# A quantised feed-forward kernel with batch-wise projection: projecting on 128 rows instead of 64, turning the weights before they are rounded, and new programs for all engines

## The reference

```python
def reference(x, itok, cond_weights, w_up, w_down):
    w = cond_weights[itok]                          # (64, 64, 64)
    z = einsum('bct,bcd->bdt', x, w)                # per sample
    h = hbitlinear(z, w_up)                         # 512 -> 1024
    h = square(relu(h))
    return x + hbitlinear(h, w_down)                # 1024 -> 512

def hbitlinear(x, w):
    x = fwht(x)                                     # Walsh-Hadamard over the last axis, / sqrt(n)
    scale = 127 / max(abs(x).max(-1), 1e-5)         # one scale per token
    xq = clip(round(x * scale), -127, 127) / scale
    s = max(mean(abs(w)), 1e-5)
    wq = clip(round(w / s), -1, 1) * s              # ternary weights
    return einsum('bsd,fd->bsf', xq, wq)
```

## Time and profile before

| | |
|---|---|
| time, median of 3 runs | 283.66 us (283.53 to 283.95) |
| the profiled execution, its span | 279.9 us |
| TensorE busy | 246.1 us (88%) |
| VectorE busy | 204.7 us (73%) |
| GpSimd busy | 181.4 us (65%) |
| ScalarE busy | 147.4 us (53%) |
| DMA moved | 34.96 MB in 67369 packets, mean 125 GB/s |

### The profile page before, as it was taken

One profiled execution on the slowest core, in us unless ns is written; L12 is line 12 of the kernel. 1 busy time (PEld: TensorE's weight loads), 2 busy tenths in 40 slices (PEclk: granted clock), 3 DMA queues, 4 the chain that ended last, 5 costly groups with the idle time before them and its releaser, 6 DMA issues.

```text
span 279.9 us, 6739 instructions
## 1 busy us (share of the span) xinstructions
PE 246.1 (88%) x2116; PEld 203.6 (73%) x2116; DVE 204.7 (73%) x341; ACT 147.4 (53%) x193; POOL 181.4 (65%) x231
## 2 busy tenths in 40 slices
PE   0266899799999999999999999999999899985872
PEld 0266797797979797979797888888888687754441
DVE  0145557799888697888878796969697977887632
ACT  2143588765647465655656565556462766641220
POOL 1333133869797979697979788887976467278510
PEclk9999999999999999999999999999999999998899
DMA  6865963245563745585664437434443325553364
GB/s 188 305 210 204 191 158 51 42 122 95 143 107 92 154 122 89 143 143 128 155 191 87 122 75 215 94 94 98 116 84 106 81 57 109 135 112 75 75 86 141
DMA packets 67369, 34.96 MB, mean 125 GB/s; under 512 B 57490, under 2 KB 57618, under 8 KB 67346
## 3 DMA queue, kind: packets, MB, share of 16 engines
q10 hardware_dynamic: 52432, 14.75, 28.4%
q1 hardware_dynamic: 14914, 19.93, 23.3%
HBM read 13.70 MB, written 8.39 MB: 79 GB/s over the span
## 4 chain that ended last, share of the span: by engine, by line
PE 61%; issue 9%; DMA 8%; POOL 6%; DVE 5%; ACTq 4%; ACT 3%; SPq 2%; POOLq 0%; DVEq 0%
PE u_ps L750 15%; PE h_ps L737 14%; PE o_ps L761 13%; PE y_ps L708 10%; PE z_ps L721 8%; DMA zqT<-zq 4%; POOL p L422 4%; ACTq L527 2%; DMA uqT<-uq 2%; ACT uq L547 2%; POOL u_deq L430 1%; DVE u_max L931 1%; ACTq L554 1%; DVE y L893 1%; DMA w_pair<-in_L_cond_weights_dram 1%
## 5 line engine op out<-in xcount | busy, mean ns | idle before, releaser
L422 POOL TENSOR_TENSOR p<-g 128x512 f32<-128x512 f32 x64 | 80.9, 1287 | 23.6 <-DVE g L924 22.9
L750 PEld LDWEIGHTS u_ps<-had_sb,p 128*128 128x128 f32 x512 | 61.0, 193 | 12.2 <-POOL p L422 7.1
L750 PE MATMUL u_ps<-had_sb,p 128*128 128x128 f32 x512 | 63.8, 278 | 6.8 <-POOL p L422 4.4
L737 PE MATMUL h_ps<-zqT,w_upT 128*128 128x256 f16 x512 | 61.8, 272 | 2.5 <-ACT g L534 1.3
L761 PE MATMUL o_ps<-w_downT,uqT 128*128 128x512 f16 x256 | 61.7, 384 | 2.4 <-DMA uqT<-uq 2.4
L385 POOL TENSOR_TENSOR x_half<-x_all 128x512 f32<-128x512 f32 (+1 forms) x32 | 40.9, 1300 | 25.9 <-PE y_ps L708 15.3
L737 PEld LDWEIGHTS h_ps<-zqT,w_upT 128*128 128x128 f16 x512 | 49.4, 98 | 9.5 <-issue 2.0
L547 ACT ACTIVATE uq<-u_ps,u_mul 128x1024 f16<-128x1024 f32 x32 | 35.6, 1114 | 34.2 <-DVE u_mul L944 28.2
L534 ACT ACTIVATE g<-h_ps 128x512 f32<-128x512 f32 x64 | 37.7, 595 | 21.8 <-PE h_ps L737 10.1
L931 DVE TENSOR_REDUCE u_max<-u_ps 128x1 f32<-128x1024 f32 x32 | 39.0, 1218 | 10.8 <-PE u_ps L750 10.7
L708 PE MATMUL y_ps<-w_pair,x_half 64*128 64x64 f32 x512 | 35.4, 293 | 12.1 <-DMA w_pair<-in_L_cond_weights_dram 12.1
(11 more groups left out here) (35 smaller groups left out, 142.1 us busy)
## 6 DMA issues: line engine op xcount, KB each, us to landing
x_all<-in_x_dram SPq DMA_DIRECT2D x32, 256.0 KB, 3.3
out_dram<-out_sb SPq DMA_DIRECT2D x32, 256.0 KB, 2.3
w_raw<-in_L_ffn_w_up_dram ACTq DMA_DIRECT2D x4, 512.0 KB, 4.4
w_raw<-in_L_ffn_w_down_dram SPq DMA_DIRECT2D x4, 512.0 KB, 4.9
w_pair<-in_L_cond_weights_dram SPq DMA_DIRECT2D x64, 16.0 KB, 2.2
zqT<-zq ACTq DMA_TRANSPOSE x32, 2.7
uqT<-uq ACTq DMA_TRANSPOSE x32, 3.1
had_sb<-in_hadamard_dram ACTq DMA_DIRECT2D x1, 64.0 KB, 3.6
```

The source lines that it names most:

```text
L422: nc.gpsimd.tensor_tensor(new[:, :, m, :], old[:, :, 0, :], old[:, :, 1, :], (ALU.add, ALU.subtract)[m]).then_inc(s_p8[k], 1)
L737: mm = nc.tensor.matmul(h_ps[u % 2][:, i, :], w_upT[:, q, f * P:(f + 1) * P], zqT[par][:, q, :], start=(q == 0), stop=(q == TC - 1))
L750: mm = nc.tensor.matmul(u_ps[:, c * P:(c + 1) * P], p8[par][:, c, k * P:(k + 1) * P], had_sb[:, :], start=True, stop=True)
```

## The change

- **Projection.** x is loaded in another layout: `x_half` now holds the left 256 columns of a sample's 64 rows on partitions 0 to 63 and the right 256 on partitions 64 to 127. The gather writes a sample's matrix twice, to both halves of the partitions, as `w_pm[:, 0]`; a new VectorE operation, `w_sign`, makes `w_pm[:, 1]` with the lower half negated. One matmul over 128 rows with 128 columns moving then gives the sum and the difference at once. There are 8 such matmuls per tile in place of 16, and `x_outer` is gone. The first four of them (l = 1) have a semaphore of their own, on which `y_split` waits.
- **x twice.** `x_all` is gone. `residual` reads x from `x_res`, a ring of two per half, loaded by a second set of transfers (`load_xr`). `x_half` and `w_pm` are rings of four.
- **Weights.** `weight_turn` turns the raw fp32 chunk; `weight_round` reads the turned chunk from PSUM and writes fp16 into `w_upT` or `w_downT`; `weight_clip` (VectorE) clips it there in place. Odd chunks of the up matrix use `h_ps` as the buffer for the turn, the others `u_ps`.
- **Scales.** `z_col`, `kappa` and `out_unit` are rings of four, `u_deq` of two. `keep_z` and the two copies of `token_units` are gone.
- **Programs.** There is no loop any more: every engine's program is one flat list, and the order is new throughout.

```diff
         def project(t, half, par):
-            for h in range(2):
-                pe.wait_ge(s_xh[h], t + 1)
-            pe.wait_ge(s_wc[par], LOADED * (half + 1))
-            for h in range(2):
-                for l in range(2):
-                    for j in range(KP):
-                        for b in range(2):
-                            rows = slice(b * C, (b + 1) * C)
-                            mm = nc.tensor.matmul(y_ps[:, b, l, h, j, :],
-                                                  x_half[h][rows, j, l * P:(l + 1) * P], w[rows, j, :], ...)
-            mm.then_inc(s_y, 1)
+        def project(t):
+            pe.wait_ge(s_x[t % X_RING], LOADED * (i + 1))
+            pe.wait_ge(s_wpm, t + 1)
+            for l in (1, 0):
+                for s in range(NS):
+                    mm = nc.tensor.matmul(y_ps[:, l, :, s, :], x_half[t % X_RING][:, s, l * P:(l + 1) * P],
+                                          w_pm[t % W_RING][:, :, s, :], start=True, stop=True)
+                mm.then_inc((s_y, s_yo)[l], 1)
...
+        def gather_w(t, s):
+            after(sp, s_y, t - W_RING + 1)
+            row = sp.value_load(cond_sb[0:1, b:b + 1], min_val=0, max_val=S_SETS - 1)
+            sp.dma_start(w_pm[t % W_RING][:, 0, s, :], w_cond[bass.ds(row, 1), :, :].to_broadcast([2, C, C]))
+        def load_xr(t, k):
+            after(sp, s_out[k], t - R_RING + 1)
+            sp.dma_start(x_res[k][t % R_RING][:, :]..., x_pairs[:, KP * t + k:KP * t + k + 1, :])
+        def w_sign(t):
+            w = w_pm[t % W_RING]
+            nc.vector.tensor_scalar(w[:, 1, :, :], w[:, 0, :, :], sign[:, 0:1], None, ALU.mult)
...
-            nc.scalar.activation(w_int[n][u], w_raw[n][:, u * WQ:(u + 1) * WQ], ACT.Copy, scale=w_inv[:, n:n + 1])
+            act.wait_ge(s_wturn[n], u + 1)
+            nc.scalar.activation(dst, src, ACT.Copy, scale=w_inv[:, n:n + 1])      # src in PSUM
-                mm = nc.tensor.transpose(w_ps[u % 2][:, i * P:(i + 1) * P],
-                                         w_int[n][u][:, i * P:(i + 1) * P], ident[:, :])
+                mm = nc.tensor.transpose(dst[:, i * P:(i + 1) * P],
+                                         w_raw[n][:, u * WQ + i * P:u * WQ + (i + 1) * P], ident[:, :])
+        def weight_clip(n, u):
+            nc.vector.tensor_scalar(part, part, UNIT, -UNIT, ALU.min, ALU.max)     # fp16, in SBUF
...
-                in1=x_all[:, bass.ds(t * KP + k, 1), :].rearrange("p o t -> p (o t)"),
+                in1=x_res[k][t % R_RING][:, :],
```

1934 lines of the change are left out of this document (1234 added, 700 removed).

## The result

The changed kernel takes 318.61 us (median of 4 runs, 316.77 to 321.60) against 283.81 us of the kernel before on the same chip: a ratio of 1.1237, with a 95% interval of 1.1155 to 1.1319. It is slower by 35 us; 281.2 was forecast, with 289 as the upper end. The profiled execution took 316.77 us; its span is 314.9 us, 35.0 more than before. Some executions of every kernel here, of the one before too, take some per cent longer at a lower granted clock; the ratios leave them out.

A forecast was written before the change was run, and what follows sets the result against it. TensorE was taken to bound the filled middle, with losses at both ends. 279.9 - 2.9 - 2.5 + 3.6 + 1 - 2.3 = 276.8 us; the 3.7 offset gives 280.5, and 0.7 for a missed wait 281.2; range 275 to 289.

The forecast's parts named there:

- The projection: TensorE's projection falls from 1.93 to 1.78 us and the down behind it by 0.10; -2.9 us over eleven tiles.
- Raw turns: Fp32 weight turns before the first had_u: one record each, +4 us of TensorE work; two records (rival, 0.12), +11.
- The head: Start up to the first had_u: it begins at 55 us with two up more done; -2.5 with one stall less.
- 7.67 1.72 x2: SyncE's gathers at the start: two take 1.72 us, so tile 0's last goes out by about 6.7.
- the same 2.7 us to land: Tile 0's last gather lands as fast as before; with w_sign, the first projection starts at 10.0 us.
- Waits of the new order: TensorE stops for late turns at down(11,1) 2.4, down(7,1) 1.2, down(9,0) 1.0 and down(10,0) 0.7 us; term +3.6.
- one missed: Allowance of 0.7 us, the price of the smallest named wait, for a wait of the new order not found.
- The prediction's own sign of being wrong: The forecast is wrong if TensorE idles over 6 us in the middle, or if turns take two records.
- ScalarE's order becomes the bound: Rival, chance 0.22: late turn_u and quant_z on ScalarE hold TensorE, 288 us; decided from a landing of some 3.7 us.
- DMA: SyncE's queue carries 12,288 packets more, 19% more on 52% in the middle; room, but turns may land later: +1 us.
- The tail: Near the end, TensorE's 3.15 us wait for GpSimd's g_last of tile 14 mostly goes: -2.3 us.

The follow-up runs named there:

- e15: Kernel before's order, weights rounded before turning, 128-row projection, x loads issued by GpSimd and spaced out, tile 1's w_sign behind tile 0's maximum; ratio 1.0096 to the kernel before.
- e8: e6 with gathers from fixed rows and without their register loads; only its rest is given, 221 to 224 us.
- e9: e6 with the 64 loads of x issued by GpSimd instead of SyncE; only its rest is given, 221 to 224 us.
- e11: e6 with both edits of e9 and e10: x loaded by GpSimd, weights rounded before they are turned; 295.7 us.
- e17: e15 with the weights turned raw, so all of the change's data paths in the order of before; ratio 1.0691 to the kernel before.
- e2: The changed kernel with SyncE's list sorted by when TensorE needs each transfer; ratio 1.1338 to the kernel before.
- e6: The change's data paths with the kernel before's order on TensorE, ScalarE, GpSimd and VectorE, and SyncE's list by deadline; ratio 1.0894 to the kernel before.
- e1: The changed kernel with gathers from fixed rows, without SyncE's register loads; ratio 1.0772 to the kernel before.
- e7: The changed kernel unaltered, run again on the same chip as e5 and e6; 314.93 us, ratio 1.1049 to the kernel before.
- e18: The changed kernel in its own order, with e15's loads of x (by GpSimd, spaced); ratio 1.1402 to the kernel before.
- e5: The changed kernel with 23 turn_u moved up ScalarE's list, each right behind the operation following its own quant_u; 323.90 us.
- e10: e6 with the weights rounded before they are turned, as in the kernel before; its two quickest executions took 298.31 and 300.63 us.

## Why the prediction was wrong

**The projection: right.** 1.79 us a tile (1.78 forecast), and the `down` behind it lost its 0.10. Three lines of e15's chain of waits, and a projection of it 14.09 us from the next in the timeline:

```profile
160.87 1.79 PE y_ps L877 x16
162.66 1.73 PE o_ps L933 x8
...
172.34 1.73 PE o_ps L933 x8
```

```profile
146.62 1.95 PE L877 MATMUL y_ps<-w_pm,x_half 128*128 128x128 f32 x16
160.71 1.95 PE L877 MATMUL y_ps<-w_pm,x_half 128*128 128x128 f32 x16
```

Both `down` now take 1.73. By the rule on draining in the Trainium skill (TensorEngine Tiling (Array Packing), Key Properties) this was to be expected, and the trace agrees with it. A tile at 14.09 against 14.34, over eleven tiles, is the -2.9 of the sum to 0.2 us; but it needs a middle without waits, which only e8, e9 and e11 to e17 had.

**Raw turns: right in the unit, wrong in the term.** One record, 0.87 us for eight. Eight ordinary fp32 matmuls of this shape make 16 records and take 1.78. So a turn costs half. The Trainium skill (TensorE: Matmul & The Clock Gate, Terms) speaks of a transpose mode four times as fast for fp32; the trace shows a factor of two, whether or not these turns use that mode, and the measurement decides. `w_sign` took 0.35 (0.3 forecast).

**The head: two steps failed at its start, the issue of the gathers and their landing.** "7.67 1.72 x2" was taken for the price of two gathers. It holds two issues and one register load. A gather cost 1.26 us in the kernel before and costs 1.83 in its new form (2.1 in the first set), not 0.86, so the last of tile 0 was out at 10.87 instead of 6.7. And "the same 2.7 us to land" became 5.7, with two loads of 512 KB let out just ahead by ScalarE's new order, which the sum did not look at; that they are the cause is likely by e2 and e6, but not tested alone. Without register loads (e1) the start gained only 0.9 us, so a right price of the gathers alone would not have saved the term. The first projection began at 17.03 instead of 10.0, which is 7 us of the 11.5; further on TensorE waited 3.5 us for zqT and 3.8 for x. The head ended at 66.55 instead of 55: the term of -2.5 measured +11.5 (+8.2 in e7).

**Waits of the new order: the named ones came, the sum of the others was missed, and this is the step that cost most.** The term was +3.6, and TensorE was without work for 19 us more than before in the rest. `down(11,1)` waited 2.35 (2.4 forecast), `down(9,0)` 0.91 (1.0), `down(7,1)` 0.35 (1.2), `down(10,0)` nothing (0.7). I had allowed 0.7 for "one missed". Missed were `down(0,0)` 2.49, `down(12,1)` 1.40, `down(13,1)` 1.34, `down(15,0)` 4.64 and all waits for other operands: from the first `had_u` on 33 us without work, against 14. The prediction's own sign of being wrong was over 6 us idle in the middle. The rival "ScalarE's order becomes the bound" had the place and the sign, and its point of decision, a landing of 3.7 us, was passed (4.2). But it priced four waits at 7 us; e17 and e18 make the order's price 20. Its premise that every `down` before had about a whole tile of cover holds for half of them only: counted in the two programs at the unit prices above, the order of before gives `down(t,0)` 10.6 us and `down(t,1)` 14.1 us of TensorE's work behind their `had_u` in every tile from 1 to 9, while the change gives anything from 8.8 to 15.9, with the same median within 1.4 us. Maximum, two small steps, `quant_u`, turn and landing need 1.2 + 0.5 + 1.1 + 1.25 + 4.2 = 8.3 us of it, with every engine free at once. That irregularity, not a smaller mean, is the difference is an argument, not a result. Moving ScalarE's turns alone did not cure it (e5), and which rows of the order cost most stays open.

**DMA: +1 forecast, 12.6 and 13.5 us measured** in the order of before (e6 against e9, e10 against e11), though the engines had room: q1's share rose from 23.3 to 34.8%, not to the 42 that follows from 19% more at the same price. The failed step was to ask whether the bytes fit, and not who issues them when. The same bytes cost nothing in the rest once GpSimd issued x; that it is five transfers let out in 4 us around a turn that cost is read from places like the one in e6. In the order of the change the same cure won nothing (e18).

**The clock was not in the sum.** Several waits of 2.4 to 4.6 us were followed by matmuls at up to twice their time (3.59 for 1.90 at 303.59, 2.98 for the 1.95 of a projection at 61.27), though not each (1.90 at 264.13, behind 2.35); the mean granted clock fell from 0.994 to 0.956. In the rest TensorE was busy 215.19 us, against 207.94 in e15, which has two `up` (1.75 us) more to do there: by an estimate from these rows the slower stretches cost 9 us, beside the 19 of the waits themselves.

**The tail: the wait that was to go went, and was outweighed.** TensorE no longer waits for GpSimd there (before 3.15 us), but the last twenty microseconds hold the 4.64 us above.

A version that beats the kernel before was not found: e15, the projection alone with its loads spaced, is 1.0% slower. In its profiled execution, 2 us over its median, the rest is 1.1 us shorter than before and the head 6.8 us longer: the second projection waits until 24.6 us (before it began at 19.9), behind gathers of twice the bytes; what part their width has in this was not tested.
